# Twenty-two unread TensorE products placed ahead of six waits of a fused conv, attention and expert kernel

## The reference

```python
x = x + _L0_conv_ref(_gn(x), ...)     # deformable 3x3 convolution: offsets, four-corner sampling, sum
x = x + _L1_conv_ref(_gn(x), ...)     # 3x3 convolution, mixed over 4 streams by a Sinkhorn matrix (20 rounds)
t = _to_tokens(x)                     # 8 x 256 tokens of 64 numbers
t = t + _L2_attn_ref(_ln_t(t), ...)   # causal attention, 8 heads of 64, one image a batch
t = t + _L2_ffn_ref(_ln_t(t), ...)    # 8 experts of width 256, GELU, the best two by a gate
t = t + _L3_attn_ref(_ln_t(t), ...)   # gated mean over a window of 16 tokens
t = t + _L3_ffn_ref(_ln_t(t), ...)    # 16 experts of width 128, silu(h1) * h2, the best two
```

## Time and profile before

| what | value |
|---|---|
| median of three runs | 490.76 us |
| the profiled execution, own time | 486.73 us |
| its span, first to last instruction | 484.9 us |
| mean granted TensorE clock | 0.982 |
| TensorE busy | 434.6 us, 90% of the span |
| VectorE busy | 347.4 us, 72% |
| ScalarE busy | 283.1 us, 58% |
| GpSimd busy | 175.6 us, 36% |

### The profile page before, as it was taken

One profiled execution on the slowest core, in us unless ns is written; L12 is line 12 of the kernel. 1 busy time (PEld: TensorE's weight loads), 2 busy tenths in 40 slices (PEclk: granted clock), 3 DMA queues, 4 the chain that ended last, 5 costly groups with the idle time before them and its releaser, 6 DMA issues.

```text
span 484.9 us, 9115 instructions
## 1 busy us (share of the span) xinstructions
PE 434.6 (90%) x2998; PEld 303.3 (63%) x2998; DVE 347.4 (72%) x1090; ACT 283.1 (58%) x676; POOL 175.6 (36%) x305
## 2 busy tenths in 40 slices
PE   2999999999968988979999988999989888998994
PEld 1787777767467887979898944344435444545542
DVE  4178998867777656788978853637666888797862
ACT  3467776732557876758788855765655333343431
POOL 4400001203134563383793342415341454343342
PEclk9998999999989998989999999999999999999998
DMA  7300000000400000012300004212112213041330
GB/s 178 144 2 1 2 0 1 1 2 0 87 3 1 1 2 1 2 39 51 69 20 3 1 3 141 63 39 68 43 38 74 68 45 105 28 122 66 99 102 11
DMA packets 13567, 20.94 MB, mean 43 GB/s; under 512 B 4592, under 2 KB 6384, under 8 KB 13008
## 3 DMA queue, kind: packets, MB, share of 16 engines
q1 hardware_dynamic: 13056, 19.99, 14.4%
q10 hardware_dynamic: 464, 0.37, 0.3%
HBM read 19.62 MB, written 0.72 MB: 42 GB/s over the span
## 4 chain that ended last, share of the span: by engine, by line
PE 63%; DVE 16%; ACT 8%; issue 6%; POOL 4%; DMA 2%; POOLq 0%; DVEq 0%; SPq 0%; ACTq 0%
PE PS L2171 14%; PE PS L1871 7%; PE PS L1909 6%; PE PS L2182 5%; PE PS L2193 5%; PE PS L1930 3%; PE PS L2103 3%; PE PS L2091 2%; PE PS L1829 2%; PE PS L1998 2%; PE PS L2013 2%; PE PS L2047 2%; ACT score_arena L968 2%; DVE QL L1468 2%; DVE score_arena L1577 2%
## 5 line engine op out<-in xcount | busy, mean ns | idle before, releaser
L2171 PE MATMUL PS<-YTs,WH 64*128 64x512 f32 x192 | 77.0, 427 | 1.9 <-ACT VV L1067 1.6
L735 POOL TENSOR_TENSOR pr<-pr 128x512 f32<-128x512 f32 x39 | 50.4, 1291 | 75.9 <-DVE pr L1630 44.7
L2171 PE MATMUL PS<-YX,WH 64*128 64x512 f32 x192 | 77.2, 426 | 0.0
L968 ACT ACTIVATE score_arena<-score_arena,nmx 128x128 f32<-128x128 f32 (+1 forms) x128 | 56.9, 446 | 22.2 <-DVE nmx L1577 21.8
L1067 ACT ACTIVATE VV<-PS 128x512 f32<-128x512 f32 x64 | 35.4, 595 | 41.6 <-PE PS L2171 41.5
L1023 ACT ACTIVATE stage<-PS,wk 128x512 f32<-128x512 f32 x64 | 40.8, 684 | 22.8 <-PE PS L2171 22.7
L1743 DVE TENSOR_TENSOR stage<-VV,PS 128x512 f32<-128x512 f32 x64 | 41.8, 682 | 17.1 <-ACT VV L1067 12.5
L2171 PEld LDWEIGHTS PS<-YTs,WH 64*128 64x128 f32 x192 | 35.3, 184 | 29.6 <-ACT VV L1067 12.6
L908 ACT ACTIVATE st_mem<-PS 128x512 f32<-128x512 f32 x72 | 37.3, 612 | 18.5 <-PE PS L1909 18.5
L2103 PE MATMUL PS<-cst,score_arena 128*128 128x128 f32 x192 | 34.4, 290 | 6.6 <-ACT score_arena L968 6.1
L2091 PE MATMUL PS<-YTs,QH 128*128 128x128 f32 (+1 forms) x128 | 38.9, 328 | 0.0
(11 more groups left out here) (277 smaller groups left out, 1130.1 us busy)
## 6 DMA issues: line engine op xcount, KB each, us to landing
QH<-gate_store SPq DMA_DIRECT2D x96, 128.0 KB, 2.9
stage<-in_wexp SPq DMA_DIRECT2D x6, 512.0 KB, 5.9
wk<-in_w SPq DMA_DIRECT2D x1, 1034.0 KB, 9.8
wa<-in_wat SPq DMA_DIRECT2D x1, 768.0 KB, 8.1
out<-X SPq DMA_DIRECT2D x16, 32.0 KB, 1.9
cst<-in_consts SPq DMA_DIRECT2D x1, 483.0 KB, 6.4
wc<-in_w SPq DMA_DIRECT2D x2, 183.5 KB, 5.8
score_arena<-in_wcv SPq DMA_DIRECT2D x2, 144.0 KB, 6.2
```

The source lines that it names most:

```text
L735: nc.gpsimd.tensor_tensor(acc[:, c % 2], acc[:, c % 2], weighted[:, u % 2], ALU.add).then_inc(acc_added, 1)
L968: ins = nc.scalar.activation(PR[:, s % 3, cols], MS[:, s % 3, cols], ACT.Exp, bias=nmx[:, s % 3, qt:qt + 1], scale=-1.0, accum_out=rsum[:, ...
L2171: ins = mm(PS[:, banks[i], :], w[hs, m, tiles[i] * P:(tiles[i] + 1) * P], ys[i][hs, cs], start=(k == 0), stop=(k == 2))
```

## The change

Five calls of `keep_awake` are added, and a table for three fills. Each product is a float32 one of 128 x 128 weights and 256 columns.

- Four products into bank 3 between the scores of step 0 and those of step 1, and two more at the start of step 1, ahead of the wait for the first exponentials. This is one stretch of the program with two waits.
- Three into bank 3 ahead of fill ("xT", 2) of step 20, and five into bank 4 ahead of fill ("yA", 2) of step 25. They stand behind the other fills of the step and ahead of every wait of their own fill.
- In `transpose_y` the wait for bank 7 now stands ahead of the wait for the normalised tokens, for every fill of this kind, and for ("yD", 1) four products into bank 7 stand between the two.
- In `second_out(8)` four products go into the output bank of the unit, after the wait for that bank and before the wait for the hidden products.

That makes 22 products. No other engine gets an instruction more or less.

```diff
+AWAKE = {("xT", 2): 3, ("yA", 2): 5, ("yD", 1): 4}
 POWER_1 = 3
...
             def transpose_y(name, c):
                 at = C if name[0] == "z" else 0
                 yts[0] += at == 0
+                take(name, c)
+                keep_awake(7, AWAKE.get((name, c), 0) if name == "yD" else 0, 2 * P)
                 pe.wait_ge(y2_ready, yts[0])
-                take(name, c)
...
             scores(0)
+            keep_awake(3, 4, 2 * P)
             for s in range(STEPS + 2):
+                if s == 1:
+                    keep_awake(3, 2, 2 * P)
                 if 1 <= s <= STEPS:
...
                     for what in attention_fills(s):
+                        keep_awake(3 + s % 2, AWAKE.get(what, 0), 2 * P)
                         if what[0] in ("q", "v"):
...
                 u = UNITS2 + r
                 pe.wait_ge(combined, u - 1)
+                if r == 8:
+                    keep_awake(OUT_BANKS[u % 2], 4, 2 * P)
                 pe.wait_ge(prod3_done, 2 * r + 2)
```

## The result

Over 22 runs of each the changed kernel took 491.98 us (490.11 to 494.75) and the kernel before 490.02 us (485.26 to 491.81). The ratio is 1.0057, with a 95% interval of 1.0035 to 1.0078: slower by 0.57%, or 2.8 us. The forecast was 492.4 us and slower. The profiled execution of after took 490.56 us against 486.73, with a span of 488.7 us and a mean clock of 0.982. The ratios of this document leave out the runs that lie more than 1.5% above the fastest of their kernel, which in the last group of experiments are five of before's 35 runs, those with the lowest clock; the medians and ranges count every run.

A forecast was written before the change was run, and what follows sets the result against it. TensorE, with a record open for 90% of the span, was taken as the bound. The terms -0.3 - 1.45 + 1.6 + 0 + 1.75 = +1.6 us, added to the median, gave 492.4 us, range 489.4 to 494.2.

The forecast's parts named there:

- Sum: All five places together: +1.6 us, added to the median of the runs for 492.4 us.
- The likeliest case: The prediction's own forecast: 492.4 us, slower, own range 491.3 to 493.3 us, chance 0.45.
- The price of a product: One unread product on TensorE at full clock: 0.44 us, bounds 0.2 and 1.02 us.
- C: Five products at fill ("yA", 2) of step 25: no wait to fill, plain delay, +1.6 us.
- A: Six products at steps 0 and 1: fit into TensorE's waits and keep the clock up, -0.3 us.
- E: Four products before the output of unit 8: no wait there, everything behind pushed back, +1.75 us.
- B: Three products at fill ("xT", 2) of step 20: fit into a 1.80 us wait, stop the slow stretch, -1.45 us.
- D: Four products at fill ("yD", 1): fit into the wait for VectorE's tokens, nothing gained or lost, 0 us.
- rival 4: Clock falls at A anyway, 492.7 us; or delays bring a fall behind the 407 us wait, 494.0 us; chance 0.08.
- Rival 3: Faster: D and E stop clock falls behind the waits at 362 and 407 us, 489.3 us; chance 0.12.
- the forecast's 0.45: Chance given to the prediction's own forecast, half of it counted as slower by more than 1.47 us.
- The 4.03 us: Gap of the runs' median above the profiled execution's own time, 486.73 us; the profile didn't say why.

The follow-up runs named there:

- e3: Kernel before plus only the four products ahead of the output of unit 8; 491.41 us, ratio 1.0022.
- e6: Kernel before plus only four products ahead of the output of unit 10, inside its wait; 489.97 us, ratio 1.0004.
- e10: Kernel before plus only six products ahead of fill ("yB", 0) of step 30; 490.18 us, ratio 1.0034.
- e2: Kernel before plus only the five products ahead of fill ("yA", 2) of step 25; 492.04 us, ratio 1.0043.
- e8: Kernel before plus only eight products, in place of four, ahead of the output of unit 8; 493.31 us, ratio 1.0111.
- e7: Kernel before plus only the products at steps 0 and 1 and at fill ("xT", 2) of step 20; 487.92 us, ratio 0.9995.
- e5: Kernel before plus only the four products ahead of fill ("yD", 1); 489.49 us, ratio 1.0001.
- e9: Kernel before plus products at A and B and six ahead of fill ("yB", 0) of step 30, none in the experts; 488.04 us, ratio 0.999.
- e11: Kernel before plus only the products at D and four ahead of the output of unit 10; 487.98 us, ratio 1.0016.
- e4: Changed kernel with C's products moved to step 30 (six) and E's to the output of unit 10 (four); 487.85 us, ratio 0.9944 to before.
- e12: As e4, plus one product ahead of each of four short waits in units 8 and 22; 485.46 us, ratio 0.9945 to before.
- e1: Changed kernel without the products of C and E, keeping those at A, B and D; 488.26 us, ratio 0.9955 to before.

## Why the prediction was right

- **Sum.** Forecast +1.6 us on the profiled execution; measured +3.83. The five places alone make -0.37 - 1.58 + 1.62 + 0 + 1.98 = +1.65, as forecast; the rest are the parts without products (-0.34 and -0.2), the new fall at 409 (+1.53) and the end (+1.1). In the timed runs it was +2.0 us between medians and 2.8 by the ratio. The likeliest case held, and 491.98 us is 0.4 from it. Part of that closeness is luck: the forecast went up from a median of 490.76 over three runs, which over 22 runs was 490.02. From there the sum gives 491.6.
- **The price of a product.** Taken at 0.44 us. The records stand 0.216 us apart, so 0.43 a product. From the first record of a group to the next work, five took 2.22 us at C, four took 1.53 at A (the scores start at 136.74) and 1.93 at E. What makes E the dearest is not shown.
- **A.** Forecast -0.3, measured -0.37, and -0.35 to -0.38 in the five experiments that fill A as well. The waits left are 0.28 + 0.32 = 0.60 us, under the 0.7 named. Without the fall the chain of after runs through the Sinkhorn rounds of VectorE and GpSimd there. The gain is not the same in each execution: the fall cost 0.37 in before and 0.3 in e3, nothing in e6 and e10, where it came 0.5 us later against the work, and some 1.2 in e2 and e8, where it lasted 6.8 us.
- **B.** Forecast -1.45, measured -1.58. The fall at B is there in six of the eight traces that leave B empty and cost 1.2 to 1.6 us. e2 and e8 have none, so a timed run need not have this gain.
- **C.** Forecast +1.6, measured +1.62 in after and +1.63 in e2. The transposes of step 26 start at 197.70, 0.62 before those of the earlier trace rows; all up to A had given 0.71, so this is within the 0.3 us named. No wait stands before the five: they follow the last value product at once, at 195.05. The slow stretch of step 30 stayed.
- **D.** Forecast 0, measured 0: the fill starts 0.18 us behind TensorE's products and the shift is the same on both sides. That the clock behind D was 1.00 in before was a draw: five of the eight traces that leave D empty have a fall there, and it cost e2 1.6 us and e7 1.5. e5 shows no effect of D alone on the time.
- **E.** Forecast +1.75, measured +1.98 in after and in e3, and 3.7 for twice the products in e8. TensorE doesn't wait there, as forecast.
- **A mark that failed.** "I am wrong if ... the clock is slow behind D or E in one of the two traces": it is, at 409 us, and costs 1.53 us. This is rival 4's second half, and it was not in the sum. But it isn't E's doing alone, since e5 and e9 have the same fall at the same place without E. Rival 3, that E holds the clock over to unit 10, is refuted by after and e3 both. A smaller slip: half of the forecast's 0.45 is 0.22 and not 0.25.
- **The 4.03 us that the prediction left open.** 0.74 of it is the median of three runs against that of 22. Most of the rest are falls that the profiled execution did not have. Its clock was 0.982; before's timed runs beside the experiments had 0.975, 0.979 and 0.978 in the mean over the runs compared. Among these runs time and clock go together (correlation -0.91 to -0.93 in each group), by 1.3 to 1.4 us for each 3.4 us of low clock. The 18 of them with a clock of 0.982 took 486.3 to 488.9 us, 487.5 in the median. So some 2.5 us up to 490.02 go with the clock, and 0.8 between 486.73 and 487.5 stay open; after's median is 1.42 above its own profiled time too, at equal clock.

What stays open is the worth of each place by itself. The Trainium skill, in "TensorE: Matmul & The Clock Gate", section "What's actually happening", has the monitor run freely; the runs fit that: B's wait is empty in before, e2 and e3, and the fall behind it is there in before (187.89) and e3 (187.69) and missing in e2. A place is worth at most its fall, 1.6 us or 0.33%, and only in the executions that have it, while the ratios of e5, e6, e7 and e11 are known to 0.3 or 0.4% either way: these runs can neither show nor exclude such a gain. That a filled wait drives its fall to another one is not shown either. e4, e6 and e7 have falls at new places (446; 400 and 452; 361, 399 and 450), but e8, which fills none of the waits, has falls at 361, 399 and 454 as well. That filling all of them works is shown by e12, in the spread of its runs above all; the ratios of e4 and e12 (0.9944 and 0.9945) don't differ, so the worth of its short waits is argued from e4's fall at 446 alone.

## What to carry to other kernels

Put unread work only where the trace shows the engine waiting at that very instruction: two places without a wait (C and E) cost 3.6 us and turned a gain of 0.45% (e1) into a loss of 0.57%. Look for the wait itself, not for the slow stretch behind it. And read several runs' clocks before counting on a fall: where it comes is not fixed. The kernels with a gain that is clear of the noise (e1, e4, e12) fill A, B and D at least and add nothing where no wait is; with fewer of them the gain, if there was one, was lost in the spread. And look at who else is at work behind the wait: at step 30 a full clock gave 0.2 us, since GpSimd was the one waited for. Judge such a change by the spread of the runs as well as by their median.

## What the runs showed of the hardware

- The clock also fell behind waits much shorter than the 1.80 to 2.97 us of the earlier trace rows. In e6, e7, e8 and e9 it fell between 397.85 and 400.37 us, behind the two fills of unit 8. Timeline of e6 there, where the fall comes at 400.37:

```profile
397.57 0.63 PE L2000 MATMUL PS<-cst,Y 128*128 128x128 f32 x4 [0.94 <-DVE Y L1439]
398.89 0.62 PE L2028 MATMUL PS<-sw,YTs 128*128 128x32 f32 x4 [0.69 <-ACT YTs L1001]
```

E's products start 2 us behind these waits and end some 6 us ahead of unit 10's, so they fill neither; e12 puts one product ahead of each fill and has no fall there.

- Ahead of the last instructions a low stretch lasted 3.4, 6.8 or 10.2 us. In e5 TensorE was busy for 10.30 of 10.30 us at 0.50.
- What a fall costs depends on who sets the pace. A stretch of 3.4 us cost 0.2 at step 30, where GpSimd does (before, beside the traces without the fall), and 0 to 0.4 at A, where VectorE and GpSimd do in turn, but 1.2 to 1.6 at B, D and unit 10, where TensorE does. At step 30 one of 6.8 us cost 1.7 (e1, e6, e7, e11) and one of 10.2 us 3.3 (e5).
- Before's runs with a clock of 0.986 in the last group took 485.3 to 486.2 us, as long as e12's at 0.995: filling the waits took away the slow executions, it did not make the best one faster.
- The spread of this kernel's runs goes with the clock: 6.8 us over the 30 runs of before that the last ratio counts, 1.8 us over e12's 12.
